# A graph-attention layer on one core: edge loads of 256 rows instead of 128, two small operations and 32 comparisons given to GpSimd

## The reference

```python
Wh = (h @ W.T).reshape(n, K, OUT_DIM).transpose(1, 0, 2)
score_src = jnp.einsum('knd,kd->kn', Wh, a1)[:, :, None]
score_dst = jnp.einsum('knd,kd->kn', Wh, a2)[:, None, :]
e = jax.nn.leaky_relu(score_src + score_dst, 0.2)
e = jnp.where((adj == 0)[None, :, :], -jnp.inf, e)
alpha = jax.nn.softmax(e, axis=-1)
h_prime = jnp.einsum('kij,kjd->kid', alpha, Wh)
x = _layernorm(x + h_prime.transpose(1, 0, 2).reshape(n, 128), axis=-1)
```

## Time and profile before

| | us |
|---|---|
| three runs | 1410.83, 1414.08, 1414.72 |
| median | 1414.08 |
| the profiled execution's own time | 1412.29 |
| its span in the profile | 1410.2 |
| busy: DVE | 1329.6 (94%) |
| busy: ACT | 1284.4 (91%) |
| busy: POOL | 1247.2 (88%) |
| busy: PE | 1204.7 (85%) |

### The profile page before, as it was taken

How to read it: one execution, slowest core, us unless ns; L and a number is a source line. 1 busy time by engine, 2 the same in 40 slices (tenths; PEclk the granted TensorE clock), 3 DMA queues, 4 the chain that set the end, 5 groups by cost and what they waited for, 6 DMA issues and landing times.

```text
span 1410.2 us, 76980 instructions
## 1 busy us (share of the span) xinstructions
PE 1204.7 (85%) x35173; PEld 1167.1 (83%) x35173; DVE 1329.6 (94%) x1564; ACT 1284.4 (91%) x1375; POOL 1247.2 (88%) x1319
## 2 busy tenths in 40 slices
PE   7047689989999988989898989989898989999886
PEld 7037679888888988889898988989888989888886
DVE  7966689999999999999999999999999999999988
ACT  3799999999999999989999999999999999999552
POOL 1697869999999999989999999999999999999662
PEclk9568999999999999999999999999999999999998
DMA  8214556666766676666667676666756666666630
GB/s 167 63 31 41 47 72 63 66 88 63 98 55 97 56 99 62 63 88 64 95 56 98 63 71 87 64 91 64 100 54 95 64 70 87 63 78 63 74 38 25
DMA packets 55839, 101.61 MB, mean 72 GB/s; under 512 B 5721, under 2 KB 18393, under 8 KB 55513
## 3 DMA queue, kind: packets, MB, share of 16 engines
q0 software_dynamic: 36864, 67.13, 53.9%
q1 hardware_dynamic: 18648, 29.56, 6.4%
HBM read 293.67 MB, written 4.33 MB: 211 GB/s over the span
## 4 chain that ended last, share of the span: by engine, by line
PE 34%; issue 19%; DVE 15%; ACT 14%; POOL 11%; DMA 2%; DVEq 0%; POOLq 0%; ACTq 0%
PE bank L770 30%; ACT kept L456 14%; POOL kept L350 9%; DVE rest L615 8%; DVE kept L606 4%; PE bank L756 3%; DMA edge<-in_adj 2%; POOL edge L346 1%; DVE late L626 1%; DVE late L628 1%; DVE late L630 0%; POOL y L374 0%; DVE stats L655 0%; DVE mv L660 0%; DVEq L605 0%
## 5 line engine op out<-in xcount | busy, mean ns | idle before, releaser
L456 ACT ACTIVATE kept<-s_two,sd 128x1024 uint8<-128x1024 f32 (+1 forms) x1152 | 1180.3, 1115 | 67.4 <-PE bank L770 43.4
L350 POOL TENSOR_SCALAR kept<-s_two,sd 128x1024 uint8<-128x1024 f32 (+1 forms) x896 | 968.6, 1096 | 70.6 <-DVE rest L615 33.6
L606 DVE TENSOR_TENSOR kept<-bank,kept 128x1024 int32<-128x1024 int32 x512 | 600.8, 1211 | 41.7 <-issue 30.3
L770 PE MATMUL bank<-G,kept 128*128 128x66 f16 x16384 | 555.5, 193 | 72.9 <-DVE kept L606 43.3
L615 DVE TENSOR_TENSOR rest<-kept,bank 128x1024 int32<-128x1024 int32 x512 | 598.9, 1208 | 17.0 <-PE bank L770 16.7
L770 PE MATMUL bank<-F,rest 128*128 128x66 f16 x16384 | 569.8, 194 | 44.8 <-issue 23.3
L770 PEld LDWEIGHTS bank<-G,kept 128*128 128x128 fp8e4 x16384 | 526.8, 97 | 84.4 <-DVE kept L606 47.9
L770 PEld LDWEIGHTS bank<-F,rest 128*128 128x128 fp8e4 x16384 | 527.6, 98 | 65.5 <-issue 26.5
L756 PE MATMUL bank<-identb,edge 128*128 128x128 bf16 x2048 | 158.1, 220 | 54.2 <-ACT G L453 43.4
L756 PEld LDWEIGHTS bank<-identb,edge 128*128 128x128 bf16 x2048 | 119.4, 98 | 56.1 <-ACT G L453 43.7
L346 POOL DMA_DIRECT2D edge<-in_adj x256 | 150.5, 589 | 15.1 <-DMA kept<-in_x 15.1
(11 more groups left out here) (73 smaller groups left out, 318.8 us busy)
## 6 DMA issues: line engine op xcount, KB each, us to landing
edge<-in_adj POOLq DMA_DIRECT2D x256, 256.0 KB, 5.2
s_two<-sT_scratch SPq DMA_DIRECT2D x30, 512.0 KB, 4.8
kept<-in_x SPq DMA_DIRECT2D x16, 256.0 KB, 5.6
y<-in_x SPq DMA_DIRECT2D x16, 256.0 KB, 4.9
out<-y SPq DMA_DIRECT2D x16, 256.0 KB, 2.4
s_two<-sT_scratch SPq DMA_DIRECT2D x2, 256.0 KB, 3.5
y<-sT_scratch SPq DMA_DIRECT2D x1, 256.0 KB, 3.8
late<-sT_scratch SPq DMA_DIRECT2D x1, 256.0 KB, 5.0
```

Source lines behind the costliest of these rows:

```text
L350: return nc.gpsimd.tensor_scalar(out, scores, STEEP, d_steep[:, j, h:h + 1], ALU.mult, ALU.add)
L456: return nc.scalar.activation(out, scores, ACT.Sigmoid, scale=STEEP, bias=d_steep[:, j, h:h + 1])
L606: nc.vector.tensor_tensor(kept[:, r, both(q, q)[0]], edgeT[q % NT], kept[:, r, both(q, q)[0]], ALU.bitwise_and).then_inc(step_set, 1)
L770: last = nc.tensor.matmul(acc[k][:, col:col + BC], matrix[:, u, b * P:(b + 1) * P, e], values[:, q * IB + u * E + e, h].rearrange("p s c - ...
```

## The change

- A chunk's edges come by two transfers of 256 rows (`load_edges(c, u)`, two rows a partition), at the steps `t % 8` in (1, 3). POOL issues 128 transfers instead of 256, four of them ahead of the loop.
- ACT takes a third tile in 6 of a group's 32 steps instead of 8. That is two comparisons a group, 32 in all, from ACT to POOL.
- The maximum of the denominator moves from DVE to POOL, behind the sum at step 9 (except in the last group's end, which stays on DVE). POOL waits there for its own sum. DVE's reciprocal waits for `den_set` in its place.
- Epsilon is added on POOL ahead of the power. DVE keeps the negative mean.

```diff
-    EDGE_UNITS = (1, 2, 3, 4)
+    EDGE_UNITS = (1, 3)
...
-        n_act = 3 if t % 4 == 1 else 2
+        n_act = 3 if t % 16 in (1, 5, 11) else 2
...
-            def load_edges(c, b):
+            def load_edges(c, u):
...
-                nc.gpsimd.dma_start(edge[:, c % NC, b], adj_v[c // (PAIRS // CP), c % (PAIRS // CP), :, b // E, b % E]
+                nc.gpsimd.dma_start(edge[:, c % NC, u * E:(u + 1) * E], adj_v[c // (PAIRS // CP), c % (PAIRS // CP), :, u]
...
                     nc.gpsimd.tensor_tensor(sum_G, sum_G, sum_F, ALU.add).then_inc(top_set, 1)
+                    pool.wait_ge(top_set, g + 1)
+                    nc.gpsimd.tensor_scalar(rden[:, :, :], sum_G[:, :, D_OUT].rearrange("p (b h) -> p b h", h=HEADS),
+                                            TINY, None, ALU.max).then_inc(den_set, 1)
...
                 pool.wait_ge(var_set, done(g + 1))
-                nc.gpsimd.tensor_tensor(rstd[:, :], mv[:, :, 1], half_t[:, :], ALU.pow).then_inc(rstd_set, 1)
-                pool.wait_ge(rstd_set, g + 1)
+                nc.gpsimd.tensor_scalar(rstd[:, :], mv[:, :, 1], EPS, None, ALU.add).then_inc(rstd_set, 1)
+                pool.wait_ge(rstd_set, 2 * g + 1)
+                nc.gpsimd.tensor_tensor(rstd[:, :], rstd[:, :], half_t[:, :], ALU.pow).then_inc(rstd_set, 1)
+                pool.wait_ge(rstd_set, 2 * g + 2)
...
-                dve.wait_ge(top_set, g + 1)
-                then(nc.vector.tensor_scalar(rden[:, :, :], sum_G[:, :, D_OUT].rearrange("p (b h) -> p b h", h=HEADS),
-                                             TINY, None, ALU.max))
-                wait_last()
+                if g + 1 == GROUPS:
...
+                else:
+                    dve.wait_ge(den_set, g + 1)
                 nc.vector.reciprocal(rden[:, :, :], rden[:, :, :]).then_inc(rden_set, 1)
...
-                nc.vector.tensor_scalar(mv[:, :, 1], mv[:, :, 1], EPS, None, ALU.add)
                 nc.vector.tensor_scalar(minus_mean[:, :], mv[:, :, 0], -1.0, None, ALU.mult).then_inc(var_set, 1)
...
-                    pe.wait_ge(edge_loaded[c % NC], 16 * IB * (c // NC + 1))
+                    pe.wait_ge(edge_loaded[c % NC], 16 * U * (c // NC + 1))
```

More of the change, by code:

```diff
@@ L215, in gat_layernorm @@
         top_set = sem("top_set")
+        den_set = sem("den_set")
         rden_set = sem("rden_set")
@@ L340, in _ @@
                                     base=0, pattern=[[-1, P]], channel_multiplier=1).then_inc(consts_set, 1)
-            def load_edges(c, b):
-                if c >= NC and b == 0:
+            def load_edges(c, u):
+                if c >= NC and u == 0:
                     pool.wait_ge(transposed, (c - NC + 1) * CQ)
-                nc.gpsimd.dma_start(edge[:, c % NC, b], adj_v[c // (PAIRS // CP), c % (PAIRS // CP), :, b // E, b % E]
+                nc.gpsimd.dma_start(edge[:, c % NC, u * E:(u + 1) * E], adj_v[c // (PAIRS // CP), c % (PAIRS // CP), :, u]
                                     ).then_inc(edge_loaded[c % NC], 16)
@@ L383, in _ @@
             for c in range(NC):
-                for b in range(IB):
-                    load_edges(c, b)
+                for u in range(U):
+                    load_edges(c, u)
             pool.wait_ge(d_part_set, 1)
@@ L631, in take_sums @@
                 last.then_inc(acc_taken, 1)
[L633 removed]
+            CHAIN0, CHAIN_STEP = links[0], 2
             def finish(g):
@@ L644, in wait_last @@
                     dve.wait_ge(dve_chain, CHAIN0 + g * CHAIN_STEP + got[0])
-                dve.wait_ge(top_set, g + 1)
-                then(nc.vector.tensor_scalar(rden[:, :, :], sum_G[:, :, D_OUT].rearrange("p (b h) -> p b h", h=HEADS),
-                                             TINY, None, ALU.max))
-                wait_last()
+                if g + 1 == GROUPS:
+                    dve.wait_ge(top_set, g + 1)
+                    then(nc.vector.tensor_scalar(rden[:, :, :], sum_G[:, :, D_OUT].rearrange("p (b h) -> p b h", h=HEADS),
+                                                 TINY, None, ALU.max))
+                    wait_last()
+                else:
+                    dve.wait_ge(den_set, g + 1)
                 nc.vector.reciprocal(rden[:, :, :], rden[:, :, :]).then_inc(rden_set, 1)
@@ L662, in finish @@
                 wait_last()
-                nc.vector.tensor_scalar(mv[:, :, 1], mv[:, :, 1], EPS, None, ALU.add)
                 nc.vector.tensor_scalar(minus_mean[:, :], mv[:, :, 0], -1.0, None, ALU.mult).then_inc(var_set, 1)
-                assert got[0] == CHAIN_STEP
+                assert got[0] == CHAIN_STEP + (g + 1 == GROUPS)
             def per_row(v, width):
```

## The result

The changed kernel takes 1470.76 us in the median (1467.74 to 1483.54, six runs); the kernel before took 1412.45 beside it (1409.18 to 1415.54, six runs). The ratio is 1.043, with a 95% interval of 1.0393 to 1.0466: 4.3% slower, where 1405 us had been forecast and the range ended at 1420. The profiled execution took 1467.74, 55.5 more than the one of before. Now and then a run is in a slower state, and the ratios in this document leave such runs out, while the medians in us hold all runs.

The account below looks back on a forecast made before the run. The prediction took ACT to bound group 0 and DVE the other 15 groups. Its terms summed as 1412.3 - 2.2 - 4.2 - 2.3 + 1.1 + 0.2 = 1404.9, forecast 1405 us, with an 8-in-10 range of 1392 to 1420.

Parts of the forecast that it names:

- The landing: Arrival of the edge transfers for PE: same rows moved, second transfer issued one step earlier than the fourth was; cost nothing.
- the cover: PE's 4.8 us of waits for edges cost nothing, since DVE had no wait in a group where PE had one.
- The edge loads on POOL: Sixteen issues a group on POOL become eight; DVE still covers POOL up to 1.02 us an issue, so 0.
- D: Unknown price in us of POOL's issue of a 256-row transfer: between 0.59 and 1.18, taken as 0.98.
- The first rival: POOL becomes the bound because a 256-row issue costs more than 1.02 us; up to 1422 us, chance 0.17.
- The comparisons: Two comparisons a group from ACT to POOL: -2.2 us in group 0, where ACT is the bound, 0 elsewhere.
- The maximum: Maximum leaves DVE in 15 groups: -4.2 us, with the new wait for `den_set` costed at nothing.
- Epsilon: Epsilon leaves DVE in 16 groups; its hold by POOL passes to the negative mean, so only -2.3 us.
- The second rival: The hold on DVE goes with the epsilon, gaining 15.9 us instead of 2.3: 1391 us, chance 0.13.
- The end: POOL's added epsilon stands in the chain from the last statistics to the last store: +0.2 us.
- PE takes over: Third rival: PE is the next bound everywhere, DVE's 6.5 us go to waits for PE; about 1410 us, chance 0.15.
- The chance of slower: Slower by over 0.3%: 0.11, from 0.09 of the POOL-bound case and 0.02 for PE waiting for larger transfers.

Follow-up runs that it names:

- edges_only: The kernel before with only the edge loads changed to two transfers of 256 rows: 1470.17 us, ratio 1.0389.
- no_edges: The kernel before with no edge loads behind the first two chunks, so attention uses wrong edges: 1385.9 us, beside 1408.31.
- comps_only: The kernel before with only the 32 comparisons moved from ACT to POOL: 1427.42 us, ratio 1.0145.
- ops_comps: The changed kernel with the edge loads of before, four of 128 rows at steps 1 to 4: 1427.2 us, ratio 1.0094 against before.
- ops_only: The kernel before with only the maximum and epsilon moved to POOL: 1420.05 us, ratio 1.0007.
- mean_on_pool: The kernel before with the maximum, epsilon and the negative mean all on POOL: 1410.79 us, ratio 1.0023.
- place_moved: The kernel before with loads at steps 0 to 3 and ACT's third tile one step earlier, keeping the issue distances: 1414.55 us, ratio 1.002.
- edges_together: The kernel before with both transfers of 256 rows issued back to back at step 1: 1448.44 us, one run.

## Why the prediction was wrong

- **The landing, the step that failed.** It says "The rows moved are the same" and "I cost it at nothing", with the 4.8 us of PE's waits for edges as the price if the cover went. The rows and the bytes are the same. What I left out is what else goes through the DMA engines. PE's own instructions do, and the page of before had both rows:

```profile
q0 software_dynamic: 36864, 67.13, 53.9%
...
q8 instruction: 275, 4.51, 1.3%
```

  Beside them stood PE's 52.5 us of waits for "issue", the largest of PE's waits, a row that asked for a mechanism, and I had none for it. The term is +58.0 us of DVE waiting for PE in place of 0. edges_only and no_edges show its cause from both sides: the larger loads alone bring PE's wait to 132.3, and without edges it is 0.5. PE's waits for the edges themselves, which I had priced, went away.
- **The edge loads on POOL: right.** D is 0.766, between the 0.59 and 1.18 given and below both the 0.98 taken and the 1.02 from which POOL would bind. The first rival didn't come.
- **The comparisons: right in group 0.** -2.6 us for -2.2, and ACT stays the bound. For the other groups I put 0, and with before's loads that is too little: comps_only and ops_comps are 1.5% and 0.9% slower than before, by waits of DVE for PE and not for POOL.
- **The maximum: right in size on DVE, worth nothing in time.** DVE's `rden` goes from 4.0 us to 0.2, without a wait for POOL. POOL's takes 0.274, about the 0.3 given. In ops_only the gain does not show in the time.
- **Epsilon: the mechanism right, the size not.** The hold did move to the negative mean: its median went from 0.156 to 1.292 us. The Trainium skill's page "SBUF — State Buffer", section "Who interferes with whom", counts `tensor_scalar` among the operations of VectorE that can contend with GpSimd for the ports they share. The traces agree: on POOL itself the same operation takes 0.249 in the median in mean_on_pool. But the hold isn't of a fixed size. Beside before's 20.6 us DVE spends 18.4 in after, -2.2 for the -2.3 forecast, and 22.6 in ops_only, +2.0. So that after comes so near is in part luck. The second rival, that the hold goes, didn't come.
- **The end: about right.** From the start of the last negative mean to the end of the program it is 1410.2 - 1404.4 = 5.8 us in before and 1465.9 - 1459.8 = 6.1 in after, for +0.2.
- **PE takes over: the right engine for another reason.** I let PE be the next bound with its busy time, 72.8 us, and so priced it at DVE's 6.5 us, and at +1.1 in the forecast. In after's middle group PE is busy for 71.9 us and waits for instructions at three lines:

```profile
PE bank L778 <- issue: 11.5, 8, 2.0
...
PE bank L791 <- issue: 1.7, 1, 1.7
...
PE bank L764 <- issue: 1.0, 1, 1.0
```

  71.9 + 11.5 + 1.7 + 1.0 = 86.1, about the 85.0 us of the group (the durations overlap a little). PE is the bound there, by its waits and not by its work. In before the same sum is 72.8 + 1.6 + 0.3 = 74.7 of 78.7, from the waits of that group:

```profile
PE bank L770 <- issue: 1.6, 3, 0.9
...
PE bank L756 <- issue: 0.3, 1, 0.3
```

- **The chance of slower.** 0.02 of it stood for "PE waiting for the larger transfers", which is what happened in a form that I had not thought of; it was too little for a step whose cover I had looked at on one side only.

## What to carry to other kernels

A kernel of many small instructions, as this one with 70346 on PE, lives on a stream of instruction fetches, and here these share the DMA engines with its data. Before large transfers are merged or moved, look at an engine's waits for "issue" beside the table of queues, and cost what a longer unbroken stretch of data does to a fetch: here it was 4% of the time with the same bytes. More than the length of one transfer, the edges issued and not yet moved when a fetch falls due went with its delay, up to some 3.5 us of it. When a load is issued from the program order of a busy engine, the work between two issues sets their distance, and moving other work on that engine (32 comparisons) moves the loads with it.

## What the runs showed of the hardware that I had not expected

- PE's 70346 matmuls and weight loads come in 275 fetches of 16 KB. PE's wait for them is 0.5 us without edge traffic, 52.5 in before and 89.6 in place_moved with four transfers 2.8 us apart, 137.8 with two of twice the size.
- The length of a single transfer does not decide it: 128 rows twice in a row (137.9) are as bad as 256 once (132.3). Nor does the whole burst: with 11.4 us of edges in one (edges_together) the longest delay of a fetch is 4.5 us, in after 4.6.
- The granted clock falls behind PE's stalls: to 0.5 for 3.4 us, nine times behind group 0 in after, each after PE had stood still for 1.7 to 2.5 us.
- An issue on POOL grows little with the rows: 0.766 us for 256 against 0.589 for 128.
- A small DVE operation beside POOL's comparisons can be held for 2.5 us (ops_only), longer than the 1.45 that before had shown.
